# Layer 0 of a graph network kernel: one 128-edge tile of each round fetched by TensorE from a bf16 table, from round 4 on

## The chip, the cores and the metric

One core of one Trainium2 chip. The metric is the device time of one execution in microseconds. Before the change the median of 3 runs is 3726.49 us (3724.31 to 3727.02). The profiled execution took 3724.54 us, and its span (first to last instruction) is 3722.8 us.

## The reference

There are N = 6250 nodes with 96 features and 200,000 edges, sorted by their destination `dst`; `src` is random. Layer 0 is graph attention, layer 1 a weighted sum of neighbours:

```python
# layer 0
h = x @ W
e = leaky_relu((h @ att_src)[src] + (h @ att_dst)[dst], 0.2)      # self loops added
e = exp(e - segment_max(e, dst)[dst])
x = layernorm(x + tanh(segment_sum(h[src] * e / segment_sum(e, dst)[dst], dst) + bias))
# layer 1
g = gelu(x @ W_pre + b_pre)
x2 = x + segment_sum(g[src] * edge_attr, dst)
x = layernorm(x + x2 + gelu(gelu(x2 @ W1 + b1) @ W2 + b2))
```

## The kernel before, in words

Edges are taken in **groups** of 1024: 8 **tiles** of 128 edges, one edge per partition. There are 196 groups; five of them (slots 0 to 4, five buffers of everything) make a **round**, numbered 0 to 38, and group 195 stands alone at the end. `groups()` writes the order of every engine: here the first two rounds stand alone, then a hardware loop runs up to round 17, round 18 stands alone, a second loop runs to round 37, and round 38 and the last group stand alone. Because `dst` is sorted, the destinations of a group lie in a short window of nodes: 40 columns wide up to round 18 and 72 columns wide after it.

**Fetching rows.** A group needs the table row of each edge's source: 98 numbers (96 features, a one and the source's attention term). GpSimd (POOL in the profile) fetches them by indirect DMA, 8 to a group, one for each tile (L690, and for the first rounds its neighbours). Before that, SyncE's queue loads the group's `src` and `dst` (`load_edges`, L563 and L565), and for that it waits on `e0.free`, that is until the group five earlier has been summed.

**Working on a group in layer 0** is a chain over three engines, one group after the other:

- ACT (`weights`, `away`, `given`): turns the destinations into distances from the window (`far_dst` L744, eight squares L747), writes 0.2 times the scores to PSUM (L767), copies the new maxima (L769), copies the source terms from the fetched rows (L760: this one waits for the rows of the next group), and takes the exponentials (fade L776, onehot L777). L760 of the next group stands ahead of L777 of this one.
- DVE (`attend`, L1331 on): scores (L1339), maxima over the tiles (L1309), scores plus the destination's term (L1344), the maximum across partitions (L1318), its diagonal (L1319), leaky relu (L1350), candidates, new maximum, the sum of the group before (L1357, and L1359, which frees that group's slot), shifted scores (L1361), peak (L1363). Then comes L1339 of the next group.
- PE (`attend`, L999 on): sums the rows of a group, weighted, into a window of `p_acc0`: four tiles (L995), then a transposition (L989) and a broadcast (L991) of the next group's maxima, which wait for DVE, then the other four tiles (L995).

**The middle.** When the sum of 384 nodes is complete, `middle` finishes layer 0 for them and computes their rows of the table of layer 1. It stands at the end of a round, between the last group of the round and the first of the next, on all three engines (DVE begins it with L1423); a table of due times made at run time tells after which rounds. `p_node` is PSUM bank 6 and `p_node2` bank 7.

**Layer 1** already has two ways to fetch: 7 tiles of each group by GpSimd, and the eighth (the "booked" tile) by TensorE. For that the table is held in SBUF as three bf16 parts that add up to the fp32 value. DVE compares the 128 source numbers of each of the five booked tiles with the node number of each partition (L1505, 642 columns), which gives 0/1 matrices for a block of 128 nodes, and PE multiplies them with the block's three parts (L1086, 288 columns); 49 blocks cover all nodes, and DVE adds the three parts of the result (L1521).

Of the kernel before, what the change touches and what calls it, by code (L numbers as in the profile page):

```python
# [23 lines left out]
INT32 = mybir.dt.int32  # L24
# [6 lines left out]
P = 128  # L31
# [14 lines left out]
HOTS = 2  # L46


def gnn(nc, x, src, dst, edge_attr, w0, att_src, att_dst, bias0, w_pre, b_pre, w1, b1, w2, b2, out):
# [39 lines left out]
    with ctx:  # L89
# [125 lines left out]

        pair = ctx.enter_context(nc.psum_tensor("pair", [P, 2, 512], FP32))
# [61 lines left out]
        class Edge:  # L278

            def __init__(self, n):  # L280
                self.src = sems(f"e{n}_src", SLOTS)
                self.dst = sems(f"e{n}_dst", SLOTS)
                self.attr = sems(f"e{n}_attr", SLOTS)
# [4 lines left out]
                self.v = sem(f"e{n}_v")  # L288
# [16 lines left out]

        h_zero = sem("h_zero")
# [22 lines left out]
        p_top, p_topb, p_newp = bank[0][0:WIN, 0:P], bank[1][:, 0:WIN], bank[1][:, P:P + WIN]  # L329
# [5 lines left out]
        p_node, p_node2 = bank[6], bank[7]  # L335
# [55 lines left out]
        def groups(eng, body, after_round=None, alone=0):  # L391
# [11 lines left out]
            with eng.Fori(SLIM_ROUNDS, ROUNDS - 1) as it:  # L403
                one(it, WIN, WIN)
            one(ROUNDS - 1, WIN, WIN)
            return body(LAST, ROUNDS, 0, (WIN,))

        def named(it, u, ws):
            return f"{u}_{ws[0]}_{isinstance(it, int)}_{it is ROUNDS}_{first(it)}_{second(it)}"
# [7 lines left out]
        def due(eng, k, body, packed=None):  # L417

            if packed is None:
                packed = due_chunks(eng, k)  # L420
# [31 lines left out]
        def gathered(g, it):  # L452

            return 16 * (TILES * it + (LAST_T if g is LAST else TILES))

# [24 lines left out]
        def piece(c):  # L480

            return slice(PIECE[c], PIECE[c + 1])

# [24 lines left out]
        def _(sp):  # L508
# [43 lines left out]
            def load_edges(e, attrs):  # L552
                def body(g, it, u, ws):
# [3 lines left out]
                    if first(it) and not attrs:  # L557
                        return
                    if g is LAST:
# [7 lines left out]
                    if attrs:  # L567
                        sp.dma_start(attr[0:m, u, 0:t * D],
                                     edge_attr[bass.ds(g * GE, n), :].rearrange("(p j) d -> p (j d)", j=t))\
                            .then_inc(e.attr[u], 16)  # L570
                return body

            def load_booked(g, u):
                cut = P * (TILES - 1)
                sp.wait_ge(e1.free, g + 1)
                sp.dma_start(src_i[:, u, 0:TILES - 1], src[bass.ds(g * GE, cut)].rearrange("(p j) -> p j", j=TILES - 1))\
                    .then_inc(e1.src[u], 16)
                sp.dma_start(dst_i[:, u, 0:TILES - 1], dst[bass.ds(g * GE, cut)].rearrange("(p j) -> p j", j=TILES - 1))\
                    .then_inc(e1.dst[u], 16)
                sp.dma_start(dst_i[:, u, TILES - 1:TILES], dst[bass.ds(g * GE + cut, P)].rearrange("(p j) -> p j", j=1))\  # L580
                    .then_inc(e1.dst[u], 16)
# [36 lines left out]
            def load1(g, it, u, ws):  # L618
# [6 lines left out]
                if first(it) and u == SLOTS - 2:  # L625
                    sp.wait_ge(m_g, MCHUNKS + 1)
                    store_half(table1, m_st)
                    sp.wait_ge(m_g, MCHUNKS + 2)
# [9 lines left out]
            groups(sp, load_edges(e0, False), alone=2)  # L638
# [1016 lines left out]
```

## Time and profile before

| what | value |
|---|---|
| median of 3 runs | 3726.49 us |
| profiled execution | 3724.54 us |
| its span | 3722.8 us |
| busy in the span | POOL 2781.1 us, DVE 2438.3, PE 2393.6, ACT 1283.2 |
| layer 0, group loop | to about 1970 us |
| layer 1 | from about 1989 us |

PE is the matmul side of TensorE, PEld its weight loads. A row with xN stands for N instructions in one line; "mean ns" is the time of one. The time in brackets at the end of a timeline row is the idle time of the engine before it, with what ended it. The granted clock of TensorE is a share: 1.00 is 2.4 GHz and 0.50 is 1.2 GHz.

### The profile page before, as it was taken

What the parts mean: (1) busy time and instruction counts of PE and PEld (TensorE: products, weight loads), DVE (VectorE), ACT (ScalarE), POOL (GpSimd) and SP (SyncE); (2) the same over time, 40 slices, a digit from 0 to 9 for tenths busy, and PEclk for the clock granted to TensorE, in tenths of its full rate; (3) what the DMA queues carried; (4) which work ended last, traced back from release to release, by engine and by line L of the source; (5) the groups of instructions that cost most, each with busy time, mean ns of one, the idle gap of its engine ahead of it and who ended that gap; (6) DMA issues with size and microseconds to landing.
All of it is one profiled execution on the core that took longest, in us unless ns stands there. A gap on an engine that the chain in (4) does not pass through costs nothing.

```text
span 3722.8 us, 66966 instructions
## 1 busy us (share of the span) xinstructions
PE 2393.6 (64%) x16704; PEld 1951.7 (52%) x16705; DVE 2438.3 (65%) x6240; ACT 1283.2 (34%) x3893; POOL 2781.1 (75%) x2950
## 2 busy tenths in 40 slices
PE   6433343434344444444445988989888989999888
PEld 3333333333333333333334777777776777777776
DVE  7444444444466666566666777777777788888886
ACT  5433343434445555555553111111111221111222
POOL 7777777777777777777775777777777777777776
PEclk7555555555555555555557999999999999999998
DMA  5222221222222222222223343443334343444332
GB/s 102 43 42 42 41 44 42 44 42 43 42 43 44 43 44 43 43 44 45 44 45 99 93 94 90 95 94 94 95 91 96 93 96 91 97 95 99 93 95 70
DMA packets 351632, 254.26 MB, mean 68 GB/s; under 512 B 254125, under 2 KB 279218, under 8 KB 351387
## 3 DMA queue, kind: packets, MB, share of 16 engines
q0 software_dynamic: 94016, 146.16, 17.8%
q1 hardware_dynamic: 242753, 99.71, 11.7%
q10 hardware_dynamic: 14618, 6.14, 0.6%
q14 instruction: 215, 1.76, 0.2%
q8 instruction: 30, 0.49, 0.1%
HBM read 244.43 MB, written 7.25 MB: 68 GB/s over the span
## 4 chain that ended last, share of the span: by engine, by line
POOL 60%; issue 24%; ACT 4%; DVE 4%; PE 3%; DMA 2%; ACTq 1%; DVEq 1%; POOLq 0%; SPq 0%
POOL rows L690 60%; ACT onehot L747 1%; DMA rows<-table,src_i 1%; DMA src_i<-in_src_dram 1%; PE bank L1086 1%; ACT L790 1%; ACTq L740 0%; ACT pair L767 0%; DVE score L1361 0%; PE bank L1029 0%; PE bank L962 0%; ACT rowu L796 0%; DVE bst L1399 0%; ACT unused L790 0%; DVE newp L1352 0%
## 5 line engine op out<-in xcount | busy, mean ns | idle before, releaser
L690 POOL DMA_INDIRECT rows<-table,src_i x2850 | 2694.8, 946 | 896.0 <-issue 859.5
L1086 PE MATMUL bank<-node,hot 128*128 128x288 bf16 x9310 | 1228.4, 294 | 28.1 <-issue 16.5
L995 PE MATMUL bank<-onehot,rows 128*97 128x72 f32 (+1 forms) x3048 | 584.9, 369 | 814.9 <-ACT onehot L777 814.9
L1086 PEld LDWEIGHTS bank<-node,hot 128*128 128x128 bf16 x9310 | 932.2, 101 | 282.4 <-issue 20.9
L995 PEld LDWEIGHTS bank<-onehot,rows 128*97 128x97 f32 x3048 | 530.8, 281 | 854.4 <-issue 792.5
L1505 DVE TENSOR_SCALAR hot<-node,key 128x642 bf16<-128x642 int16 x1862 | 870.3, 539 | 130.8 <-PE bank L1086 80.0
L900 ACT ACTIVATE pair<-dst_i 128x8 f32<-128x8 int32 x196 | 35.2, 180 | 1175.3 <-DVE rows L1531 904.3
L747 ACT ACTIVATE onehot<-iota,far_dst 128x72 f32 (+1 forms) x1564 | 384.4, 328 | 23.0
L1339 DVE SCALAR_TENSOR_TENSOR other<-onehot,bank 128x576 f32<-128x576 f32 (+1 forms) x196 | 121.9, 622 | 404.1 <-ACT bank L760 335.4
L1073 PE MATMUL bank<-onehot,rows 128*96 128x40 f32 (+1 forms) x3128 | 306.8, 256 | 88.4 <-DVE rows L1536 50.6
L1073 PEld LDWEIGHTS bank<-onehot,rows 128*96 128x96 f32 x3128 | 295.8, 170 | 110.1 <-issue 88.7
L1531 DVE TENSOR_TENSOR rows<-rows,pair 128x672 f32<-128x672 f32 (+1 forms) x196 | 166.7, 851 | 148.5 <-DMA rows<-table,src_i 146.5
L1350 DVE TENSOR_TENSOR score<-score,pair 128x576 f32<-128x576 f32 (+1 forms) x196 | 122.2, 623 | 203.2 <-ACT pair L767 203.1
L991 PE MATMUL bank<-top_diag,ones 40*128 40x40 f32 (+1 forms) x392 | 132.3, 438 | 145.1 <-DVE top_diag L1319 143.6
L991 PEld LDWEIGHTS bank<-top_diag,ones 40*128 40x128 f32 (+1 forms) x392 | 97.9, 310 | 207.9 <-DVE top_diag L1319 205.9
L1309 DVE TENSOR_REDUCE top<-other 128x72 f32<-128x576 f32 (+1 forms) x196 | 192.5, 982 | 6.7
L760 ACT ACTIVATE bank<-rows 128x8 f32<-128x8 f32 x191 | 34.6, 181 | 440.9 <-DMA rows<-table,src_i 440.9
L790 ACT ACT_TABLE_LOAD x119 | 152.7, 1283 | 18.2 <-ACT rowt L811 11.1
L902 ACT ACTIVATE pair<-attr 128x768 f32<-128x768 f32 x196 | 156.2, 797 | 0.0
L769 ACT ACTIVATE bank<-newp 128x72 f32<-128x72 f32 (+1 forms) x196 | 43.4, 221 | 286.3 <-DVE newp L1352 286.3
L1526 DVE TENSOR_TENSOR onehot<-pair,iota 128x576 f32<-128x576 f32 (+1 forms) x196 | 121.2, 618 | 5.4 <-ACT pair L902 5.4
L1361 DVE TENSOR_TENSOR score<-score,bank 128x576 f32<-128x576 f32 (+1 forms) x196 | 121.0, 617 | 1.7
(204 smaller groups left out, 1931.1 us busy)
## 6 DMA issues: line engine op xcount, KB each, us to landing
attr<-in_edge_attr_dram SPq DMA_DIRECT2D x190, 336.0 KB
rows<-table,src_i POOLq DMA_INDIRECT x2850
node<-in_src_dram SPq DMA_DIRECT2D x195, 64.0 KB
attr<-in_edge_attr_dram SPq DMA_DIRECT2D x190, 48.0 KB
dst_i<-in_dst_dram SPq DMA_DIRECT2D x200, 4.0 KB
src_i<-in_src_dram SPq DMA_DIRECT2D x195, 4.0 KB
src_i<-in_src_dram SPq DMA_DIRECT2D x190, 3.5 KB
dst_i<-in_dst_dram SPq DMA_DIRECT2D x190, 3.5 KB
```

What stands on the lines that cost most here:

```text
L690: pool.indirect_dma_start(rows[:, u, j * width:(j + 1) * width], None, table, bass.IndirectOffsetOnAxis(ap=src_i[:, u, j:j + 1], axis=0))\
L747: last = act.activation(wide(onehot[:, u, :], w)[:, j, :], iota[:, bass.ds(lo, w)], ACT.Square, scale=FAR, bias=far_dst[:, u, j:j + 1])
L790: act.activation(unused[:, k:k + 1], zeros[0:1, 0:1], f)
L902: act.activation(p_attr, attr[:, u, :], ACT.Copy).then_inc(e1_fed, 1)
L991: pe.matmul(p_topb[:, 0:w], ones[0:w, :], top_diag[0:w, 0:w], start=True, stop=True).then_inc(t.topb, 1)
L995: last = pe.matmul(total[:, 0:w], rows0(u, it)[:, j, 0:D1], wide(weights, w)[:, j, :], start=j == 0, stop=j == most - 1)
L1073: last = pe.matmul(total[:, 0:w], rows1(u)[:, j, :], wide(hot, w)[:, j, :], start=j == 0, stop=j == most - 1)
L1086: last = pe.matmul(p_got[t], hot[:, c % HOTS, i, t * P:(t + 1) * P], tab[:, a, :, :].rearrange("p k d -> p (k d)"), start=a == 0, stop=a = ...
L1309: v.tensor_reduce(top[:, 0:w], other[:, 0:n * w].rearrange("p (j n) -> p n j", j=n), AX.X, ALU.max)\
L1350: st.step(v.tensor_tensor(by_half(score, w, n), by_half(score, w, n), p_slope(w, n), ALU.max))
L1505: last = v.tensor_scalar(hot[:, c % HOTS, i, :].rearrange("p (r e) -> p r e", r=3), src16[:, :, 0:ROW3], key[:, a:a + 1], None, ALU.is_equal)
L1531: return v.tensor_tensor(rows[:, u, 0:tiles * D], rows[:, u, 0:tiles * D], p_attr[:, 0:tiles * D], ALU.mult)
```

## The change

Layer 0 gets the same second way to fetch, for one tile per round: tile 7 of slot 0, in rounds 4 to 38 (35 rounds).

- **Table.** In rounds 1 and 2 the 49 blocks of the table (`x1`, 98 columns) are split into three bf16 parts, in 8 portions over 9 groups. ACT makes two copies and DVE two subtractions for each portion. They lie in `attr`, in a spare end of `x1` and in `hot`.
- **Sources.** SyncE's queue loads the 128 source numbers of the booked tile to all partitions, once a round (`load_src0`, behind the loads of slot 4), and ACT shortens them to int16 (`shorten_src0`, at the start of its slot 4). The loads of the booked group are split into 7 tiles and 1.
- **Marks.** DVE compares 128 columns with a [P, 1] scalar, once for each of the 49 blocks, in 10 pieces of 4 or 5 blocks: two pieces at the end of each group, for the round ahead (`marks0`). Two pieces have a buffer, so piece c waits until PE is done with piece c - 2 (`q_done`).
- **Matmuls.** PE multiplies each block, 294 columns, behind the second half of its window sum, two pieces to a group (`fetch0`), into bank 1.
- **Taking.** At the end of slot 4, DVE waits for the last piece and adds the three parts into the rows of the next round's slot 0 (`taken0`). ACT's L760 for that group waits for it.
- GpSimd gathers 7 tiles in place of 8 for that group.
- Around it: `p_topb` and `p_newp` move to bank 0, `p_node2` to bank 6 beside `p_node`, with a wait of PE on the previous chunk's GELU; no chunk is due before round 4; rounds 0 to 3 and the last two stand outside the loops; the scalar `key` is made before the loop.

```diff
-            with eng.Fori(SLIM_ROUNDS, ROUNDS - 1) as it:
+            with eng.Fori(SLIM_ROUNDS, ROUNDS - 1 - apart) as it:
                 one(it, WIN, WIN)
-            one(ROUNDS - 1, WIN, WIN)
+            for it in range(ROUNDS - 1 - apart, ROUNDS):
+                one(it, WIN, WIN)
...
+        def pieces_at(u):
+
+            return (0, 1) if u == SLOTS - 1 else (2 * u + 2, 2 * u + 3)
...
+                    if not attrs and u == SLOTS - 1 and in_era(era_at(it, u)):
+                        load_src0(it)
...
+            def load_src0(it):
+
+                if not first_era(it, SLOTS - 1):
+                    sp.wait_ge(q_src16, it + 2)
+                for k in range(BOOKED0):
+                    sp.dma_start(src_all0[:, k * P:(k + 1) * P],
+                                 src[src_rows(it + 2, k)].rearrange("(p e) -> p e", p=1).broadcast_to([P, P]))\
+                        .then_inc(q_src, 16)
...
-                    for j in range(TILES - (e is e1 and booked(it, u))):
+                    for j in range(TILES - (booked(it, u) if e is e1 else booked0(it, u, ws[0]))):
...
+                if booked0(it, u, w):
+                    act.wait_ge(q_out, it - FROM0 + 1)
                 act.activation(p_src, rows0(u, it)[:, :, D1], ACT.Copy).then_inc(t0.given, 1)
...
+            def split0(k):
+                if k > 0:
+                    act.wait_ge(h_rest, k)
+                    act.activation(table0_part(k - 1)[:, :, 1, :], table0_left(k - 1), ACT.Copy).then_inc(h_mid, 1)
+                if k < len(TABLE0):
+                    if TABLE0[k][2] is flat[2]:
+                        act.wait_ge(e0.free, 2 * SLOTS + SLOTS)
+                    act.activation(table0_part(k)[:, :, 0, :], table0_rows(k), ACT.Copy).then_inc(h_hi, 1)
...
+            def shorten_src0(it):
+
+                act.wait_ge(q_src, 16 * BOOKED0 * (it + 3 - FROM0))
+                if not first_era(it, SLOTS - 1):
+                    act.wait_ge(q_hot, (it + 2 - FROM0) * ERA0)
+                act.activation(src16_0, src_all0, ACT.Copy).then_inc(q_src16, 1)
...
+            def fetch0(it, u, c, n):
+
+                pe.wait_ge(q_hot, piece_no(it, u, c) + 1)
+                if c == 0:
+                    if first_era(it, u):
+                        pe.wait_ge(h_tab, len(TABLE0))
+                    else:
+                        pe.wait_ge(q_out, it + 2 - FROM0)
+                for i, a in enumerate(range(PIECE0[c], PIECE0[c + 1])):
+                    for t in range(n):
+                        last = pe.matmul(p_got0[t], hot0[:, c % HOTS, i, t * P:(t + 1) * P], table0_block(a),
+                                         start=a == 0, stop=a == NB - 1)
+                last.then_inc(q_done, 1)
...
                 window_sum(p_acc0, onehot[:, u, :], it, u, range(TILES // 2, TILES), w).then_inc(e0.acc, 1)
+                if in_era(era_at(it, u)):
+                    for c in pieces_at(u):
+                        fetch0(it, u, c, fetched_at(it, u, w))
 
             def middle(c, blocks=MB):
                 pe.wait_ge(m_col, c + 1)
+                pe.wait_ge(m_g, c + 1)
...
+            def taken0(it, n):
+
+                v.wait_ge(q_done, (it + 2 - FROM0) * ERA0)
+                for k in range(n):
+                    last = v.tensor_reduce(rows0(k, it + 1)[:, TILES - 1, :], p_got0[k].rearrange("p (k d) -> p d k", k=3),
+                                           AX.X, ALU.add)
+                last.then_inc(q_out, 1)
+
+            def marks0(it, u, c, n):
+
+                if c == 0:
+                    v.wait_ge(q_src16, it + 3)
+                if not first_era(it, u) or c >= HOTS:
+                    v.wait_ge(q_done, piece_no(it, u, c) - HOTS + 1)
+                for i, a in enumerate(range(PIECE0[c], PIECE0[c + 1])):
+                    last = v.tensor_scalar(hot0[:, c % HOTS, i, 0:n], src16_0[:, 0:n], key[:, a:a + 1], None,
+                                           ALU.is_equal)
+                last.then_inc(q_hot, 1)
...
                 if g is not LAST:
+                    if split_step(it, u) is not None:
+                        split_rest0(split_step(it, u))
+                    if u == SLOTS - 1 and in_era(it + 1):
+                        taken0(it, booked_in(it + 1, w))
+                    if in_era(era_at(it, u)):
+                        for c in pieces_at(u):
+                            marks0(it, u, c, fetched_at(it, u, w) * P)
+                if g is not LAST:
                     set_window(lo, after, (u + 1) % SLOTS)
```

## Rows read from the trace of the kernel before

**Rows 1.** Page of the profile, the chain that ended last, by engine.

```profile
POOL 60%; issue 24%; ACT 4%; DVE 4%; PE 3%; DMA 2%; ACTq 1%; DVEq 1%; POOLq 0%; SPq 0%
```

**Rows 2.** Stretches: busy us of PE, PEld, DVE, ACT, POOL; granted clock, DMA share, GB/s.

```profile
600.00:800.00 200.00, 80.84 (x396) 69.60 (x395) 90.15 (x298) 81.94 (x323) 151.37 (x160) 0.50 0.21 43
1200.00:1400.00 200.00, 84.79 (x413) 71.64 (x411) 126.11 (x317) 103.42 (x337) 151.24 (x161) 0.50 0.21 43
```

**Rows 3.** Groups of instructions by line, 1200 to 1900 us.

```profile
L690 POOL DMA_INDIRECT rows<-table,src_i x561 | 530.1, 945 | 171.0 <-issue 166.4 <-DMA src_i<-in_src_dram 4.6
...
L760 ACT ACTIVATE bank<-rows 128x8 f32<-128x8 f32 x69 | 12.3, 178 | 92.8 <-DMA rows<-table,src_i 92.8
```

**Rows 4.** Timeline, one group behind a middle, 1336.9 to 1344.5 us.

```profile
1336.94 0.76 DVE L1361 TENSOR_TENSOR score<-score,bank 128x576 f32<-128x576 f32 x1
...
1337.76 0.75 DVE L1339 SCALAR_TENSOR_TENSOR other<-onehot,bank 128x576 f32<-128x576 f32 x1
1337.90 0.67 ACT L777 ACTIVATE onehot<-score 128x576 f32<-128x576 f32 x1
...
1340.84 0.25 DVE L1319 TENSOR_SCALAR top_diag<-ident,top_col 72x72 f32<-72x72 f32 x1
...
1341.15 0.70 PE L991 MATMUL bank<-top_diag,ones 72*128 72x72 f32 x2 [0.67 <-DVE top_diag L1319]
...
1341.62 0.63 ACT L767 ACTIVATE pair<-score 128x576 f32<-128x576 f32 x1
1341.65 1.51 PE L995 MATMUL bank<-onehot,rows 128*97 128x72 f32 x8
...
1342.28 0.75 DVE L1350 TENSOR_TENSOR score<-score,pair 128x576 f32<-128x576 f32 x1 [1.19 <-ACT pair L767]
...
1344.43 0.75 DVE L1361 TENSOR_TENSOR score<-score,bank 128x576 f32<-128x576 f32 x1
```

**Rows 5.** Timeline around one middle, 1316 to 1347 us.

```profile
1316.17 0.42 DVE L1423 COPY colv<-acc 97x384 f32 x1 [0.61 <-issue]
...
1317.90 0.19 ACT L760 ACTIVATE bank<-rows 128x8 f32<-128x8 f32 x1 [3.45 <-DMA rows<-table,src_i]
...
1336.57 0.17 ACT L760 ACTIVATE bank<-rows 128x8 f32<-128x8 f32 x1
1336.65 0.23 DVE L1359 TENSOR_TENSOR acc<-acc,bank 97x72 f32 x1
...
1346.67 0.94 POOL L690 DMA_INDIRECT rows<-table,src_i  x1 [0.30 <-issue]
```

**Rows 6.** The chain that ended last, in order of time: start, us, what.

```profile
1337.04 2.10 DMA src_i<-in_src_dram
```

**Rows 7.** One line, L1423: the whole run, then 1010 to 1960 us.

```profile
L1423 DVE COPY colv<-acc x15: 360/421/579, 514.7 to 1918.5; 97x384 f32 x15
L1423 DVE COPY colv<-acc x12: 361/425/579, 1016.0 to 1918.5; 97x384 f32 x12
```

**Rows 8.** DVE's comparisons in layer 1 (timeline), and a 128-column operation with a scalar.

```profile
2603.43 5.54 DVE L1505 TENSOR_SCALAR hot<-node,key 128x642 bf16<-128x642 int16 x12 [0.28 <-issue]
...
L1505 DVE TENSOR_SCALAR hot<-node,key x1862: 526/539/551, 2007.8 to 3670.8; 128x642 bf16<-128x642 int16 x187
...
L1177 DVE TENSOR_SCALAR w0dst<-ones,w0att x1: 282/282/282, 9.3 to 9.3; 96x128 f32<-96x128 f32 x1
```

**Rows 9.** PE's table matmuls in layer 1 (timeline), early and late.

```profile
2011.36 4.85 PE L1086 MATMUL bank<-node,hot 128*128 128x288 bf16 x20 [7.29 <-DVE hot L1505]
...
3334.50 7.51 PE L1086 MATMUL bank<-node,hot 128*128 128x288 bf16 x60
```

**Rows 10.** Stretch of the same view as rows 2, at the start of layer 1.

```profile
2010.00:2020.00 10.00, 8.64 (x53) 6.16 (x54) 9.88 (x21) 3.35 (x6) 7.63 (x8) 0.70 0.60 143
```

**Rows 11.** DVE adding the three parts in layer 1, by line, 2100 to 3600 us.

```profile
L1521 DVE TENSOR_REDUCE node<-bank 128x96 f32<-128x288 f32 x175 | 69.9, 449 | 20.1 <-PE bank L1086 20.0
```

More of the change, by code:

```diff
@@ L389, in x_here, with groups @@
                 eng.wait_ge(s_x[-1], 16)
-        def groups(eng, body, after_round=None, alone=0):
+        def groups(eng, body, after_round=None, alone=0, apart=0):
             def one(it, w, then):
@@ L417, in due @@
         def due(eng, k, body, packed=None):
+            if isinstance(k, int) and k < HELD:
+                return
             if packed is None:
@@ L482, in piece, with in_era, narrow, booked_in @@
             return slice(PIECE[c], PIECE[c + 1])
+        def in_era(e):
+            return not isinstance(e, int) or FROM0 <= e < ROUNDS
+        def narrow(e, w):
+            return e < SLIM_ROUNDS if isinstance(e, int) else w == SLIM
+        def booked_in(e, w):
+            return BOOKED0
+        def booked0(it, u, w):
+            return in_era(it) and u < booked_in(it, w)
+        def loaded0(it, u, w):
+            if u >= BOOKED0 or (isinstance(it, int) and it < FROM0):
+                return 16 * (it + 1)
+            if booked0(it, u, w):
+                return 32 * it + 32 - 16 * FROM0
+            return 16 * (it + 1 + (SLIM_ROUNDS if u else ROUNDS) - FROM0)
+        def gathered0(g, it, u, w):
+            last = LAST_T if g is LAST else TILES
+            if u >= BOOKED0 or (isinstance(it, int) and it < FROM0):
+                return 16 * (TILES * it + last)
+            if booked0(it, u, w):
+                return 16 * ((TILES - 1) * (it + 1) + FROM0)
+            return 16 * (TILES * it + last - ((SLIM_ROUNDS if u else ROUNDS) - FROM0))
+        def fetched_at(it, u, w):
+            return booked_in(era_at(it, u), w)
+        def era_at(it, u):
+            return it + 2 if u == SLOTS - 1 else it + 1
+        def pieces_at(u):
+            return (0, 1) if u == SLOTS - 1 else (2 * u + 2, 2 * u + 3)
+        def piece_no(it, u, c):
+            return (it + (2 if u == SLOTS - 1 else 1)) * ERA0 + c - FROM0 * ERA0
+        def first_era(it, u):
+            return isinstance(it, int) and era_at(it, u) == FROM0
+        HELD = FROM0
+        SPLIT_AT = ((1, 0), (1, 1), (1, 2), (1, 3), (1, 4), (2, 1), (2, 2), (2, 3), (2, 4))
+        def split_step(it, u):
+            return SPLIT_AT.index((it, u)) if isinstance(it, int) and (it, u) in SPLIT_AT else None
+        def src_rows(e, k):
+            return bass.ds((e * SLOTS + k) * GE + P * (TILES - 1), P)
         class Steps:
@@ L558, in body @@
                         return
+                    if not attrs and booked0(it, u, ws[0]):
+                        load_split(g, u, e)
+                        return
                     if g is LAST:
@@ L637, in _ @@
             store_table()
-            groups(sp, load_edges(e0, False), alone=2)
+            groups(sp, load_edges(e0, False), alone=FROM0, apart=1)
             sp.wait_ge(e0.free, GROUPS + SLOTS)
@@ L693, in gather @@
                 return body
-            groups(pool, gather(e0, table0, D2), alone=2)
+            groups(pool, gather(e0, table0, D2), alone=FROM0, apart=1)
             pool.wait_ge(m_st, STORED)
@@ L861, in middle_due @@
                 table_for(ACT.Exp, 3)
-            groups(act, weights, middle_due, alone=2)
+            groups(act, weights, middle_due, alone=FROM0, apart=1)
             rest(act, middle, middle_last)
@@ L1037, in _ @@
             spread_top(t0, 1, SLIM)
-            groups(pe, attend, alone=2)
+            groups(pe, attend, alone=FROM0, apart=1)
             def unread(n):
@@ L1478, in _ @@
             v.wait_ge(s_w, 16 * 8)
+            v.tensor_copy(key[:, :], key_i[:, :])
             set_window(0, load_window(0), 0)
-            prev = groups(v, attend, middle_due, alone=2)
+            prev = groups(v, attend, middle_due, alone=FROM0, apart=1)
             left = due_chunks(v, ROUNDS)
@@ L1495, in _ @@
             v.sem_inc(f_var, 1)
-            v.tensor_copy(key[:, :], key_i[:, :])
             def marks(it, c):
```

117 lines of the change are left out of this document (91 added, 26 removed).

## The prediction

> **What bounds the kernel now.** The page's chain first: GpSimd's work and its issue gaps are 84% of the chain that ended last [rows 1]. The stretches of layer 0 show GpSimd equally busy in its narrow rounds and its wide ones, with TensorE's clock granted at 0.50 throughout, 1.2 GHz, while PE is busy 40 to 42% [rows 2]. By line, 561 indirect DMAs take 530.1 us and stand 171.0 us idle in between, nearly all of it issue [rows 3]: one per 1.25 us (1.248 below), 10.0 us for a group, 49.9 us for a round, with no wait that lasts. So GpSimd sets layer 0, and the other three engines follow it.
>
> How closely they follow is what decides. ACT's wait for fetched rows is 92.8 us over 69 wide groups [rows 3], 1.3 us a group: little. The timeline says why. A wide group that has fallen behind runs from L1361 to L1361 in 7.49 us [rows 4]: five are 37.4 us. A group with a middle in it, from L760 to L760, takes 18.67 [rows 5], so a middle adds 11.2 and such a round needs 48.6 of GpSimd's 49.9. There are 15 middles, 12 of them from 1010 us on [rows 7], in the 19 rounds 20 to 38, at most one to a round. GpSimd doesn't notice, because the slots are a cushion: behind a middle, L1359 frees a slot at 1336.88, the load of its sources lands at 1339.14 [rows 5, 6], and GpSimd comes to that slot at 1346.67 [rows 5]. The cushion is 7.5 us there.
>
> **Removed.** 35 indirect DMAs by 1.248 us: 43.7 us if GpSimd stays the bound. A round then has 39: 48.7 us.
>
> **Added on DVE.** 12 comparisons of 642 columns take 5.54 us, one alone 0.539 [rows 8]: they start 0.455 apart, 0.084 less than one lasts. A 128-column operation with a scalar lasts 0.282 [rows 8], so a column costs 0.50 ns and a mark 0.455 - 514 x 0.50 ns = 0.20 us apart. Bounds: 0.16, if a column costs half of that, to 0.28, if they don't overlap. I take 0.195: 0.98 for a piece of five, 1.95 for a group. Taking the parts is one reduction, 0.449 in layer 1 [rows 11], 0.37 with the same overlap.
>
> Of the column rate a page has more. The Trainium skill, "VectorE: DVE Perf Modes", What auto-detection actually checks, would give a 16-bit one-source operation with even outer dimensions four elements a cycle; by that rule a column costs half, marks come an estimated 0.165 us apart, and the sum below would come out about 12 us lower. No row here has that shape.
>
> **Added on PE.** 20 table matmuls take 4.85 us at the start of layer 1, 60 of them 7.51 later [rows 9]: 0.24 and 0.125 us each. The first is at the half clock, and 294 columns in place of 288 make it 0.245: 2.45 us for a group's ten. They come behind the second half of the window sum.
>
> **What lies beside and what on the path.** With GpSimd ahead, all of this hides: a narrow group has DVE busy 4.5 us in 10 [rows 2], 6.5 with the marks. Rounds 4 to 19 keep their gain: 16 x 1.25 = 20.0 us. The wide, lagging group is another matter, because the change closes a loop:
>
> - DVE's second piece of marks waits until PE is done with the second piece of the group before (two buffers), then 0.98;
> - from L1339 to the end of L1319: 1337.76 to 1341.09, 3.33 [rows 4];
> - from there PE's broadcast and second half: to 1343.16, 2.07 [rows 4];
> - ten table matmuls 2.45, and some 0.1 for semaphores. Sum 8.9 us.
>
> DVE's own loop is shorter: 3.33, from L1350 to L1361 2.15, from L1361 to L1339 0.82 [rows 4], marks 1.95: 8.2. Today DVE idles 1.19 before L1350, waiting for ACT's L767 [rows 4]; that idle time is the only cover, and it is used up. At slot 4 the reduction (0.37) and all marks wait for the fetch, some 0.8 more than elsewhere on balance. ACT's L760 for the next slot 0 waits for that reduction, and behind it in ACT's queue stand L776 and L777 of slot 4, for which PE's next first half waits; that is in the same 0.8. A plain round is 4 x 8.9 + 9.7 = 45.3 us, and a middle adds 11.2, plus 0.6 because L1423 now stands behind nine marks: 57.1.
>
> Against GpSimd's 48.7, a middle round overruns by 8.4 and a plain one gives back 3.4. With 11 middle rounds and 7 plain ones from 20 to 37 the followers never catch up, and the slots come free too late: GpSimd stalls. Round 38 has nothing left to fetch (48.6). The stretch costs 11 x 57.1 + 7 x 45.3 + 48.6 = 993.8, where it was 19 x 49.93 = 948.7: 45.1 more. Less the 20.0: **25 us slower, if PE keeps the half clock.**
>
> It will not always. At the start of layer 1, 4.85 us of dense matmuls came before the clock rose, and PE was busy 8.64 of 10 us at a mean of 0.70 [rows 9, 10]. In a lagging group broadcast, second half, fetch and the next first half nearly touch, so the clock should rise now and then. At the full clock the loop through PE is gone, DVE's 8.2 is left, a middle round is 53 and a plain one 42, GpSimd bounds nearly everything, and the outcome is about -27: 43.7, less some 10 us of stalls behind neighbouring middles and 6 of lag at the end. I take the full clock for a quarter of the fetches: 25 - 0.25 x 52 = **12 us slower**.
>
> **Costed at nothing.** The split in rounds 1 and 2: nine steps, each two ACT copies and two DVE subtractions of up to 686 columns. The rows with 576 columns are 0.63 and 0.75 [rows 4], so about 1.5 us on each engine; the fifth slot ahead covers it, and if it doesn't, five steps cost up to 8 us. SyncE's third load and the 64 KB broadcast per round go out on an idle queue four groups early; behind them waits only the next group's load. ACT's `shorten_src0` waits for DVE's marks and then delays slot 4's squares; that ends about when DVE does. `p_node2` with its wait: the GELU is a round old. `key` moves, 0.2 us. Longer loop bodies: no row prices them; 0 to 0.5 us a round, 0 to 17 in all, taken as 0. Layer 1 is untouched.
>
> This execution took 3724.5 us, the median is 3726.5; I put the sum on the median: 3738.
>
> **Rivals.**
> 1. **The PE clock rises and GpSimd stays the bound.** For it: nearly 5 us of PE work in one piece per group, as long as the piece that brought the clock up in layer 1. Against: PE still stands idle for about a third of each group, and a faster PE is idle sooner. About 27 us faster, 3700; 36 with marks at 0.16. Chance 0.30.
> 2. **Loop and gain cancel.** Every 0.1 us in the lagging loop is 18 x 5 x 0.1 = 9 us, so a loop of 8.8 in place of 8.9, and a clock that is full somewhat more often, end within 0.2% (7.5 us, about what this measurement can tell from no change). 0.20.
> 3. **GpSimd is held up by DVE's marks.** A diagonal (L1319) or copy beside GpSimd's work stretches DVE (L1423: 360 to 579 ns [rows 7]), while GpSimd keeps its 1.25 us [rows 3]. If it were GpSimd that waited, some 1.5 DMAs a group by half a mark, 0.2 us, in the 80 groups of rounds 4 to 19: 17 more, 29 slower, 3755. This decides from 0.25 us a group on, where the gain of rounds 4 to 19 is gone. 0.08. The Trainium skill speaks for it: "SBUF — State Buffer", Who interferes with whom, says that a vector operation in a two-port mode and GpSimd fully block each other, GpSimd's descriptor writing included. The trace agrees for DVE's side and shows nothing of it on GpSimd's.
>
> **How the numbers follow.** The forecast, the lagging loop wins, has 0.42, nearly all of it slower; with rival 3 slower is 0.50, same 0.20, faster 0.30. Slow end: marks 0.22 apart at the half clock add 11 to 25, and a few us of loop code: 3766. Fast end: the full clock, 3699. The likeliest case alone runs from 3730 to 3766.
>
> **What would show it.** Right: indirect DMAs 2815 in place of 2850 on L690's group; narrow rounds of 48.7 us; from 1000 us on, GpSimd with idle time that ends with loads of `src_i`, some 45 to 65 us in all, behind middles; wide groups behind a middle at 8.9 us; marks 0.2 apart; DVE waiting for PE before its marks; ACT's wait for rows nearly gone in the wide rounds. Wrong: a granted clock well over 0.6 in the wide part with GpSimd never waiting (rival 1); indirect DMAs over 1.25 us apart while DVE marks (rival 3); lagging groups under 8.3 us.

## The result, and the profile after

The changed kernel takes 3741.26 us (median of 6 runs, 3736.41 to 3746.19), the kernel before 3725.58 (6 runs, 3724.26 to 3727.02): 15.7 us more, ratio 1.0044, interval 1.0034 to 1.0054. The profiled execution is the slowest of the six, 3746.19, so its parts add up to some 5 us too much.

First the stretches again, the same view and columns as [rows 2], changed kernel:

```profile
600.00:800.00 200.00, 126.23 (x600) 93.18 (x600) 127.88 (x504) 86.59 (x336) 151.30 (x160) 0.57 0.23 44
1200.00:1400.00 200.00, 117.73 (x597) 86.79 (x598) 156.48 (x506) 104.11 (x336) 145.77 (x154) 0.65 0.23 43
```

In the narrow stretch GpSimd is as busy as before. In the wide one it has lost 5.5 us of 151, while DVE went from 126 to 156. What GpSimd waited for, in the whole run (engine, line, what it waited for: total us, times, longest):

```profile
POOL rows L821 <- issue: 847.7, 2780, 0.3
POOL rows L821 <- DMA src_i<-in_src_dram: 56.1, 33, 6.8
POOL rows L821 <- DMA table<-rowt: 34.3, 1, 34.3
```

33 gathers waited for `src_i`, one of them for 6.8 us: the slot came free too late, so its load started too late. The groups by line, 1200 to 1900 us, to set beside [rows 3]:

```profile
L821 POOL DMA_INDIRECT rows<-table,src_i x528 | 501.4, 950 | 195.7 <-issue 155.8 <-DMA src_i<-in_src_dram 40.0
L1534 DVE TENSOR_SCALAR hot<-node,key 128x128 bf16<-128x128 int16 x646 | 117.6, 272 | 8.9 <-PE bank L1164 6.0 <-issue 1.0
L893 ACT ACTIVATE bank<-rows 128x8 f32<-128x8 f32 x67 | 11.6, 173 | 32.0 <-DVE rows L1523 32.0
L1523 DVE TENSOR_REDUCE rows<-bank 128x98 f32<-128x294 f32 x14 | 6.5, 464 | 9.4 <-PE bank L1164 9.4
```

ACT's wait for gathered rows, 92.8 us before, is gone altogether; what is left, 32.0, is a wait for DVE's reduction of the fetched tile. The followers are now the ones that are late. A lagging wide group in the timeline (start us, us), to set beside [rows 4]:

```profile
1335.80 2.66 PE L1164 MATMUL bank<-attr,hot 128*128 128x294 bf16 x10
...
1336.31 0.74 DVE L1568 TENSOR_TENSOR score<-score,bank 128x576 f32<-128x576 f32 x1
...
1337.27 0.91 DVE L1534 TENSOR_SCALAR hot<-node,key 128x128 bf16<-128x128 int16 x5
...
1338.50 0.91 DVE L1534 TENSOR_SCALAR hot<-node,key 128x128 bf16<-128x128 int16 x5 [0.32 <-PE bank L1164]
...
1339.32 0.74 DVE L1546 SCALAR_TENSOR_TENSOR other<-onehot,bank 128x576 f32<-128x576 f32 x1
...
1342.19 0.41 DVE L1494 TENSOR_SCALAR top_diag<-ident,top_col 72x72 f32<-72x72 f32 x1
...
1342.67 0.76 DVE L1557 TENSOR_TENSOR score<-score,pair 128x576 f32<-128x576 f32 x1
...
1344.18 1.92 PE L1164 MATMUL bank<-attr,hot 128*128 128x294 bf16 x7
...
1344.81 0.75 DVE L1568 TENSOR_TENSOR score<-score,bank 128x576 f32<-128x576 f32 x1
```

From L1568 to L1568 it is 8.50 us, where it was 7.49. The five marks of the second piece begin 0.32 us late, at the end of the fetch of the group before. And the idle 1.19 us that DVE had before L1350 is gone before L1557. Slot 4 of the same round, the same view:

```profile
1360.24 2.66 PE L1164 MATMUL bank<-hot 128*128 128x294 bf16 x10
...
1362.76 0.23 DVE L1570 TENSOR_TENSOR node<-cand,node 128x72 f32 x1
1362.93 0.46 DVE L1523 TENSOR_REDUCE rows<-bank 128x98 f32<-128x294 f32 x1
...
1363.49 0.19 ACT L893 ACTIVATE bank<-rows 128x8 f32<-128x8 f32 x1 [1.63 <-DVE rows L1523]
1363.61 0.24 ACT L929 ACTIVATE fade<-drop 97x72 f32<-97x72 f32 x1
1363.76 0.67 ACT L930 ACTIVATE onehot<-score 128x576 f32<-128x576 f32 x1
1364.56 0.90 PE L1150 MATMUL bank<-onehot,rows 128*97 128x72 f32 x8 [1.67 <-ACT onehot L930]
...
1368.89 0.75 DVE L1546 SCALAR_TENSOR_TENSOR other<-onehot,bank 128x576 f32<-128x576 f32 x1 [4.03 <-issue]
```

PE's ten matmuls, DVE's reduction, ACT's copy of the next group's scores, the exponentials behind it and PE's next sum stand in a row. The last row is slot 0 of the next round: DVE has stood 4.03 us, and no semaphore ended it ("issue"). The kernel before has the same wait; of DVE's waits between 1200 and 1900 us:

```profile
DVE other L1339 <- issue: 44.8, 14, 3.7
```

There GpSimd's pace hid it. Here, with the followers late, it is on the path. The trace also records branches and register operations. In those, 3.38 us of the 4.03 lie between the branch at the end of the hardware loop's body (it ends at 1365.06 us) and the loop's first register operation (1368.44), L455 both. The view of the DMA queues for 1365.1 to 1368.4 us (packets, MB, share) has this line:

```profile
q14 instruction: 2, 0.02, 1.9%
```

That is two packets of 8 KB on the queue that the profile calls "instruction". In the wide rounds each return of the loop has such a gap (the packets are those of the returns without a middle):

| | return without a middle | packets in it | return behind a middle |
|---|---|---|---|
| before | 2.71 to 2.86 us | 1 | 2.2 to 2.7 us |
| after | 3.34 to 3.73 | 2 | 2.1 to 2.7 |
| e3, few marks | 2.75 to 2.96 | 1 | 2.2 to 2.6 |

Where no loop goes back, as into rounds 19, 37 and 38 of the changed kernel, DVE doesn't stand at all before this instruction. So the wait belongs to the loop's return, and it is longer where two packets start in it. That it is the loading of instructions fits all of this, but no run tried it by itself.

ACT's copy (L760 before, L893 now) runs once a group; its ends cut every run into parts. In us, the profiled executions of this kernel, the one before and those of the experiments below:

| | start to round 4 | rounds 4 to 19 | rounds 20 to 37 | from there to layer 1's first gather | layer 1 |
|---|---|---|---|---|---|
| before | 217.8 | 800.1 | 900.0 | 70.9 | 1733.9 |
| after | 219.7 | 782.0 | 933.9 | 70.5 | 1738.3 |
| e1, narrow rounds only | 219.6 | 782.3 | 899.5 | 70.4 | 1735.4 |
| e2, five buffers | 220.1 | 783.5 | 909.0 | 70.5 | 1734.5 |
| e3, few marks | 220.3 | 781.5 | 886.9 | 70.1 | 1734.2 |
| e4, few matmuls | 219.8 | 781.5 | 897.0 | 70.4 | 1734.7 |
| e5, two tiles | 222.0 | 856.4 | 895.2 | 70.0 | 1733.8 |
| e6, double marks | 220.3 | 803.7 | 899.8 | 70.7 | 1733.9 |
| e8, taken earlier | 220.4 | 781.9 | 893.6 | 71.5 | 1737.2 |

The change lost 1.9 us at the start, won 18.1 in the narrow rounds, and lost 33.9 in the wide ones. Layer 1's 4.4 us more belong to this execution and not to the change: its indirect DMAs stand 1.2507 us apart there, 1.2484 in the run before (mean of the undisturbed distances), and e3 and e4, with the same layer 1, take 1734.2 and 1734.7.

### The profile page after: what moved, and what is told of

Same layout as the page of the kernel before. It is cut to its first block, busy times and chain, and to the rows that moved or that the text cites. A ratio compares the mean times of both kernels' runs of the same rounds, so it can differ in the third digit from the quotient of the medians.

```text
span 3744.4 us, 72954 instructions
## 1 busy us (share of the span) xinstructions
PE 2753.9 (74%) x18419; PEld 2135.9 (57%) x18420; DVE 2754.6 (74%) x8006; ACT 1327.5 (35%) x3956; POOL 2760.5 (74%) x2915
## 4 chain that ended last, share of the span: by engine, by line
POOL 47%; issue 23%; DVE 11%; PE 10%; ACT 4%; DVEq 2%; DMA 1%; ACTq 1%; POOLq 0%; SPq 0%
POOL rows L821 47%; PE bank L1164 4%; PE bank L1150 3%; DVE hot L1534 2%; DVE other L1546 2%; DVE score L1551 1%; PE bank L1146 1%; DVEq L1451 1%; ACT onehot L878 1%; ACT L943 1%; DVE top_diag L1494 1%; ACT pair L920 1%; DVE top_col L1493 1%; DMA rows<-table,src_i 1%; DVE score L1568 0%
## 5 line engine op out<-in xcount | busy, mean ns | idle before, releaser
L1150 PE MATMUL bank<-onehot,rows 128*97 128x72 f32 (+1 forms) x3048 | 532.6, 346 | 253.7 <-ACT onehot L930 253.3
L1150 PEld LDWEIGHTS bank<-onehot,rows 128*97 128x97 f32 x3048 | 490.3, 260 | 332.5 <-issue 231.2
L1534 DVE TENSOR_SCALAR hot<-node,key 128x128 bf16<-128x128 int16 x1715 | 314.5, 276 | 43.3 <-PE bank L1164 37.9
L1144 PE MATMUL bank<-ident,top 128*72 128x128 f32 x196 | 75.1, 383 | 247.0 <-DVE top L1484 246.9
L1164 PE MATMUL bank<-attr,hot 128*128 128x294 bf16 x910 | 242.7, 449 | 0.0
L1557 DVE TENSOR_TENSOR score<-score,pair 128x576 f32<-128x576 f32 (+1 forms) x196 | 122.1, 623 | 117.1 <-ACT pair L920 115.9
L1164 PE MATMUL bank<-hot 128*128 128x294 bf16 x735 | 200.4, 450 | 0.0
L1144 PEld LDWEIGHTS bank<-ident,top 128*72 128x72 f32 x196 | 31.9, 163 | 269.7 <-DVE top L1484 266.7
L1164 PEld LDWEIGHTS bank<-attr,hot 128*128 128x128 bf16 x910 | 137.6, 157 | 66.1
```

The source lines that it names most:

```text
L1150: last = pe.matmul(total[:, 0:w], rows0(u, it)[:, j, 0:D1], wide(weights, w)[:, j, :], start=j == 0, stop=j == most - 1)
L1164: last = pe.matmul(p_got0[t], hot0[:, c % HOTS, i, t * P:(t + 1) * P], table0_block(a), start=a == 0, stop=a == NB - 1)
L1534: last = v.tensor_scalar(hot0[:, c % HOTS, i, 0:n], src16_0[:, 0:n], key[:, a:a + 1], None, ALU.is_equal)
```

## The experiments

T is the theory of the forecast: GpSimd bounds the narrow rounds, the loop of the lagging group through DVE and PE the wide ones. R1: the marks' own time on DVE is the whole price. R2: DVE's marks hold up GpSimd. R3: the splits at the start and the longer code are the price.

**A chip that had to be left out.** The first four kernels ran on a chip where the kernel before took 5391.42 us in place of 3725. Both layers are slower there: e1_narrow takes 2803 us up to layer 1's first gather and 2639 for layer 1, where the same kernel elsewhere takes 1972 and 1735.

> The fetch is kept in rounds 4 to 19 (the narrow windows) and left out of rounds 20 to 38; what the change does to the start (tables, splits) stays. T, the forecast's theory (narrow rounds are bound by GpSimd, wide rounds by the lagging group's loop through DVE and PE): the 16 narrow rounds keep 16 x 1.25 = 20 us, less the 3 us that the splits at the start cost in the changed kernel's trace, and from round 20 on the kernel is that of before: 3725.6 - 17 = 3708 to 3710 us, and the idle time of GpSimd that ends with src_i is gone from 1200 us on. R2 (the marks hold up GpSimd's DMA instructions wherever they run): the narrow rounds pay too, 3725 or more. R3 (the splits and the code are the price): about 3738.

> All as in the changed kernel, but five buffers for the marks in place of two, so that no mark waits for the previous group's fetch on PE; only the first mark group after a group 4 still waits for PE, by way of taking the fetched rows. T: in the wide rounds DVE's marks wait for PE's fetch of the group before, and PE's fetch waits for the marks; with five buffers the lagging group falls from 8.2-8.5 us to DVE's own 8.0-8.2, and the interval behind slot 4 from 11.4-11.6 to about 11.2: some 36 us back in 19 wide rounds, so 3741 - 36 = 3705 us, with 15 us of GpSimd's idle time left. R1 (the marks' own time on DVE is the price, the wait for PE lies beside it): within 5 us of 3741. R2 (marks hold up GpSimd): 3741.

> One mark in place of about five for each piece, 10 in place of 49 comparisons a round; the 49 matmuls read the first mark's block of the piece, so the fetched rows are not the table's. 39 of 49 comparisons are left out, nothing else. T: DVE has 6.4 us a round less to do and PE's matmuls remain; the two buffers still make the next marks wait for PE: 3725.6 - 30 = 3696 us. R1 (marks on DVE are the whole price): the whole of the DMAs' gain comes through, 3725.6 - 41 = 3685 us. R2 gives 3685 as well, with GpSimd's DMA instructions closer together than 1.253 us. R3 (splits, code): 3735.

> One matmul in place of about five for each piece, 10 in place of 49 a round; all 49 comparisons stay, and the fetched rows are a fifth of the table's. 39 of 49 matmuls of the fetch are left out, nothing else. T: the wait of the marks for PE falls from 1.2 us a piece to 0.25; the loop of the lagging group is then DVE's own, 8.0-8.2 us, and the interval behind slot 4 is about 10.3: 3725.6 - 30 = 3696 us, 45 us under the changed kernel. R1 (marks' own time on DVE): 3736 to 3741, little change. R2 (marks hold up GpSimd): 3741, no change.

Measured: e1_narrow 5469.57 us, ratio 1.0148 [1.0104, 1.0192]; e2_five_buffers 5541.97, 1.0261 [1.0209, 1.0313]; e3_few_marks 5548.42, 1.0275 [1.023, 1.032]; e4_few_matmuls 5493.65, 1.0156 [1.0091, 1.0221]. e2 came to the same chip again:

> [...] T: in the wide rounds the loop of the lagging group runs through DVE's wait for PE's fetch of the group before; with five buffers it falls from 8.2-8.5 us to about 8.1, and the interval behind slot 4 to about 11.2. An event-by-event recount of the rounds with the marks at the measured 0.166 us and the fetch at half clock gives 22 us faster than before, some 36 us faster than the changed kernel: 3704 us, with about 15 us of GpSimd's idle time left. R1 (the marks' own time on DVE is the price): within 5 us of the changed kernel, 3736 to 3746. R2: the same as R1.

It took 5532.03 us, before 5407.44, ratio 1.0268 [1.0194, 1.0343]. What DVE waited for between 700 and 1700 us of e1_narrow there:

```profile
DVE hot L1543 <- remote: 184.6, 31, 10.2
DVE top_col L1502 <- remote: 71.5, 16, 11.8
DVE acc L1575 <- remote: 70.1, 8, 11.1
```

Up to 10 us at a time before a mark, 31 times, for something that the trace doesn't show. PE and ACT have such gaps too, up to 12 us, and GpSimd waits up to 14.7 us for `src_i`. What causes them stays open. No theory was about this, and the order of the kernels (e3, with the fewest comparisons, is no faster than e2) fits none. These five runs decide nothing; all that follow ran where the kernel before takes 3725 to 3730.

**e1: the fetch in rounds 4 to 19 only.**

```diff
-            return not isinstance(e, int) or FROM0 <= e < ROUNDS
+            return FROM0 <= e < END0 if isinstance(e, int) else not LATE[0]
```

with END0 = 20, and rounds 20 on in a loop without the fetch.

> [...] The fetch is kept in rounds 4 to 19 and left out of rounds 20 to 38. T: the narrow rounds keep 16 x 1.25 = 20 us, less 3 us that the splits at the start cost, and from round 20 on the kernel is that of before: 17 us faster than before, 3708 to 3710 us, and GpSimd's idle time that ends with src_i is gone from 1200 us on. R2 (the marks hold up GpSimd's DMA instructions): no faster than before. R3 (the splits and the code are the price): 12 us slower than before.

Measured: 3709.41 us, before 3725.31, ratio 0.9959 [0.9945, 0.9973]: 15.9 us faster than before, in T's place. In the wide rounds GpSimd and ACT are where they were:

```profile
L830 POOL DMA_INDIRECT rows<-table,src_i x562 | 530.8, 944 | 171.3 <-issue 170.1 <-DMA src_i<-in_src_dram 1.2
L902 ACT ACTIVATE bank<-rows 128x8 f32<-128x8 f32 x70 | 12.4, 178 | 90.6 <-DMA rows<-table,src_i 90.6
```

So the whole loss comes from fetching in rounds 20 to 38. R3 falls: tables, splits and much of the code are all here. By the table they cost 1.8 us at the start.

**e2: five buffers for the marks in place of two**, the others in idle columns of `node`.

```diff
-                if not first_era(it, u) or c >= HOTS:
-                    v.wait_ge(q_done, piece_no(it, u, c) - HOTS + 1)
+                if not first_era(it, u) or c >= HOTS0:
+                    v.wait_ge(q_done, piece_no(it, u, c) - HOTS0 + 1)
```

> The kernel of e2_five_buffers, this time for a chip on which the kernel before takes its 3725 us (five buffers for the marks in place of two, all else as in the changed kernel). T: 3704 us, 22 us faster than before and 36 us faster than the changed kernel, with about 15 us of GpSimd's idle time left and lagging groups of about 8.1 us. R1 (the marks' own time on DVE is the price): 3736 to 3746. R2 (marks hold up GpSimd): the same as R1.

Measured: 3718.76 us, before 3725.95, ratio 0.9981 [0.9971, 0.9991]. 22.5 us of the changed kernel's time are back, not 36: T's direction and 0.63 of its size, and R1 falls as the whole cause. GpSimd's wait for `src_i` went from 56.1 to 25.3 us, the lagging groups from 8.21 (median of the 36 in slots 1 to 3 behind a middle) to 7.95. What stayed is slot 4 (and the return of the loop, 3.4 to 3.9 us); there, in the timeline:

```profile
1055.52 1.19 PE L1174 MATMUL bank<-hot,node 128*128 128x294 bf16 x4
1055.54 0.23 DVE L1580 TENSOR_TENSOR node<-cand,node 128x72 f32 x1
1056.74 0.47 DVE L1533 TENSOR_REDUCE rows<-bank 128x98 f32<-128x294 f32 x1 [0.97 <-PE bank L1174]
1057.13 1.55 DVE L1544 TENSOR_SCALAR hot<-node,key 128x128 bf16<-128x128 int16 x9
1057.30 0.19 ACT L903 ACTIVATE bank<-rows 128x8 f32<-128x8 f32 x1 [2.59 <-DVE rows L1533]
```

More buffers don't touch this: DVE waits 0.97 us for PE's last piece, and ACT 2.59 for DVE. The interval behind slot 4, in rounds behind a middle, is 10.92 us in the median, 10.90 in the changed kernel.

**e3: a fifth of the comparisons.** One mark a piece; 39 of 49 comparisons a round are left out.

```diff
-                for i, a in enumerate(range(PIECE0[c], PIECE0[c + 1])):
+                for i, a in enumerate(range(PIECE0[c], PIECE0[c] + 1)):
```

> The kernel of e3_few_marks, for a chip on which the kernel before takes its 3725 us: 10 of the 49 comparisons a round are done and 39 are left out, all matmuls of the fetch stay, two buffers. e2_third gave back 22 us of the changed kernel's time by taking away the wait of the marks for PE; left over against the narrow-only kernel are 10 us. T: DVE's loop for a lagging group falls from 7.96 to 7.5-7.9 us (PE's matmuls remain), GpSimd's stalls are nearly gone: 30 us faster than before, 3696 us, and the tail after the last gather of layer 0 is back near 28 us. R1 (only the marks on DVE cost): 3685. R2 (marks hold up GpSimd): 3685, with GpSimd's instructions 1.250 apart in place of 1.254. R3 (splits, code): 3735.

Measured: 3694.94 us, before 3725.98, ratio 0.9915 [0.9898, 0.9931]. T's 3696; 10 us over R1's and R2's 3685. Lagging groups take 7.56 us, slot 4 still 10.67. The edit also shortens the body of the loop, and its return takes 2.75 to 2.96 us in place of 3.34 to 3.73: over 7 plain rounds that is up to an estimated 5 us of the gain, which no theory had.

**e4: a fifth of the fetch's matmuls**, two buffers, all marks; the same edit in `fetch0`, so 39 of 49 matmuls a round are left out.

> The kernel of e4_few_matmuls, for a chip on which the kernel before takes its 3725 us: 10 of the 49 matmuls of the fetch a round are done and 39 are left out, all 49 comparisons stay, two buffers. It takes away the marks' wait for PE (as e2_third's five buffers did, 3718.8 us) and also the wait of the fetched rows for PE's last pieces behind slot 4, which e2_third keeps (11.2 us there, against 9 to 10 in e1_again). T2 (that wait is a price of its own, about 0.9 us a round in 19 wide rounds): 3696 to 3705 us, the interval behind slot 4 at about 10.3 us. R1 (what e2_third left over is the marks' own time on DVE alone): 3716 to 3719 us, as e2_third.

Measured: 3705.10 us, before 3726.58, ratio 0.9941 [0.9924, 0.9958]: T2's upper end, 14 us under e2, while R1 wanted none. Lagging groups 7.96, as in e2; slot 4 at 10.14. With the marks' wait for PE away in both, the difference is slot 4, and its remaining 2.2 us over its neighbours are not PE's.

**e6: every comparison twice**, in e1's kernel, the first into blocks that nobody reads.

```diff
-                    last = v.tensor_scalar(hot0[:, c % HOTS, i, 0:n], src16_0[:, 0:n], key[:, a:a + 1], None,
+                    for k in (HOTS, 0):
+                        last = v.tensor_scalar(hot0[:, k + c % HOTS, i, 0:n], src16_0[:, 0:n], key[:, a:a + 1], None,
```

> The narrow-only kernel of e1_again (3709.4 us) with every comparison done twice, the first time into blocks that nobody reads: 784 more marks of about 0.165 us, 129 us more of them on DVE, in rounds 4 to 19, where DVE is busy 0.64 of the time and GpSimd sets the pace. T (the marks do not hold up GpSimd, and DVE has room in the narrow rounds): 3709 to 3713 us, GpSimd's instructions still 1.250 to 1.254 us apart. R2 (a mark holds up GpSimd's DMA instructions): the time rises by the share of the marks that fall into GpSimd's part of writing descriptors; if each held it for its own length, up to 129 us more, 3838; by a third of that, 3752.

Measured: 3730.06 us, before 3724.98, ratio 1.0014 [1.0004, 1.0023]: 20.7 over e1. Both missed on the time. On the mechanism, GpSimd's DMA instructions between 270 and 740 us, those that waited for a load left out, by whether a mark ran beside them:

| | with a mark: number, mean ns, over 970 ns | without |
|---|---|---|
| e1 | 105, 951, 12 | 271, 944, 0 |
| e6 | 139, 959, 34 | 225, 946, 5 |

So marks do hold GpSimd, but by little: in these 470 us the distances beside marks add 0.7 us in e1 and 2.3 in e6. R2 is real as an effect and falls as the price. The 21.4 us lie in rounds 4 to 19, and there the narrow groups have become the bound: from round 5 to 16 a round without a middle takes 49.9 to 50.5 us, its groups 11.0, 8.8, 9.1, 9.1 and 12.2. "DVE has room" was read off its busy share; its loop had none left.

**e5: two tiles a round** in rounds 4 to 19: BOOKED0 = 2, the second sum in the bank 7, which layer 0's loop leaves idle.

> The narrow-only kernel of e1_again (3709.4 us) with two tiles of each of the rounds 4 to 19 fetched by TensorE in place of one (slots 0 and 1), the second into another PSUM bank: GpSimd issues 38 DMAs a round, 47.5 us in place of 48.7; each mark has 256 columns (by four elements a cycle 0.033 us longer than 0.163), and the fetch has 98 matmuls a round, at half clock 24 us in place of 12. T: a narrow group's loop through the two buffers and PE grows by 2.45 us, from some 6.5 to 9 us, against 9.5 us that GpSimd leaves a group, so most of 16 x 1.25 = 20 us comes through: 3690 to 3696 us. Rival: the groups that lag behind the middles of rounds 9, 13 and 16 can no longer catch up, the narrow rounds become consumer-bound like the wide ones: 3709 or more, with GpSimd waiting for src_i before 1000 us.

Measured: 3778.00 us, before 3724.98, ratio 1.0145 [1.0122, 1.0169]. The rival, and far beyond its 3709; GpSimd waits 105 us for `src_i` before 1000 us, as it said. DVE's marks and what they waited for in the whole run:

```profile
L1543 DVE TENSOR_SCALAR hot<-node,key x784: 266/282/511, 167.2 to 1030.8; 128x256 bf16<-128x256 int16 x196
its engine sat idle before it (us, times) until:
  PE bank L1173: 150.0, 123
```

That is 150 us of waits for PE. Twenty matmuls a group, 4.9 us, sit in the loop through two buffers; the interval behind slot 4 is 16.15 us, and a narrow round 54.6. Slot 4 was the term that this forecast lacked.

**e8: pieces one group earlier, taken behind slot 3**, with e2's buffers and nothing left out.

```diff
-            return it + 2 if u == SLOTS - 1 else it + 1
+            return it + 2 if u >= SLOTS - 2 else it + 1
...
-                    if u == SLOTS - 1 and in_era(it + 1):
-                        taken0(it, booked_in(it + 1, w))
                     if in_era(era_at(it, u)):
                         for c in pieces_at(u):
                             marks0(it, u, c, fetched_at(it, u, w) * P)
+                    if u == SLOTS - 2 and in_era(it + 1):
+                        taken0(it, booked_in(it + 1, w))
```

> All 49 comparisons and matmuls, five buffers as in e2_third (3718.8 us), and the schedule of the fetch moved one group forward: the first pieces of a round are marked in slot 3 of the round two before, the last in slot 2 of the round before, and DVE takes the fetched rows behind the marks of slot 3 in place of ahead of those of slot 4; the shortening on ACT and the load of the indices move with it. In e2_third DVE waits 0.97 us for PE's last piece there, and ACT's rows wait for the following group ends only with DVE's taking, so that its exponentials come late: an interval of 11.16 us behind slot 4. T3 (that chain, PE's last piece to DVE's taking to ACT's rows and exponentials, is what e2_third lost): the interval falls to 7.96 + 0.45 = 8.4 us, the 18 wide rounds take from 909 us down to near GpSimd's 48.7 us each, 877 to 885, and the tail behind the last gather shrinks: 3684 to 3695 us, faster than all kernels that leave nothing out. R4 (DVE's work for marks and taking is the price, wherever it stands): no more than the 0.97 us of DVE's wait in 18 rounds come back, 3700 to 3705 us.

Measured: 3705.90 us, before 3729.83 on that chip, ratio 0.9937 [0.9924, 0.9951]: 23.9 us faster than before. In the timeline of DVE, slots 3 and 4 of a round behind a middle:

```profile
1340.61 0.75 DVE L1579 TENSOR_TENSOR score<-score,bank 128x576 f32<-128x576 f32 x1
1341.42 1.59 DVE L1545 TENSOR_SCALAR hot<-node,key 128x128 bf16<-128x128 int16 x9
1342.93 0.45 DVE L1534 TENSOR_REDUCE rows<-bank 128x98 f32<-128x294 f32 x1
1348.78 0.75 DVE L1579 TENSOR_TENSOR score<-score,bank 128x576 f32<-128x576 f32 x1
```

The reduction waits for nobody, and the interval behind slot 4 is 8.21 us, from 10.92: T3's mechanism, and close to its number for it (8.4). The time is not T3's 3684 to 3695, and nearer R4's. 4 us are the chip (its DMAs stand 1.2502 us apart, and before took 4 more). The rest is in the wide rounds: 893.6 us, where GpSimd's own pace would be 18 x 39 x 1.2502 = 877.6. Middle rounds take 51.3 to 52.5 us. Five plain rounds, each behind a single middle, take 46.5 to 47.1 and catch up with GpSimd (their slot 3 takes 9.4 to 10.4, ACT waiting for rows). The two behind a pair of middles (32 and 35) don't, and still take 45.4 and 45.0, where five groups of 7.9 to 8.5 would be about 41: slot 0 of a plain round takes 12.1 to 13.0, with this DVE wait in it:

```profile
1355.38 0.76 DVE L1557 SCALAR_TENSOR_TENSOR other<-onehot,bank 128x576 f32<-128x576 f32 x1 [4.06 <-issue]
```

Two rounds in a row with middles (30 and 31, 33 and 34, 36 and 37) are then not made up for, and between GpSimd's last gather of layer 0 and its first of layer 1 lie 35.4 us, 28.7 before. T3's sum had left this boundary out. Of the 4.06 us, 3.61 are the return of the loop, with two packets of the instruction queue in it, as in the changed kernel. A kernel without it was not tried.

## Why the prediction was right, and where it was not

3738 was predicted and 3741 measured, "slower" had 0.50, and the mechanism was the one named: narrow rounds on GpSimd, wide rounds on their followers, GpSimd stalling behind middles. The sum was better than its terms, and that is luck: rounds 20 to 37 at the half clock were put at 46.5 us more (11 x 57.1 + 7 x 45.3, against 18 x 49.93) and cost 33.9, and the 13 us that the clock was to give back did not come.

- **Narrow rounds keep 20.0.** 18.1 kept, 17.8 in e1. The splits, costed at nothing with a bound of 8, took 1.9 us.
- **Marks 0.195 apart.** The median is 0.163, near the lower bound: the column rate of the 642-column row was carried over, and it is half that here (that row reads 3 rows of 214 columns, an odd outer dimension; a mark reads 128 in one). A piece takes 0.82 us, not 0.98. This is where the Trainium skill's "VectorE: DVE Perf Modes", What auto-detection actually checks, was right against my reading of rows: the estimate from it was 0.165. e5's 256-column marks last 0.282 us where the 128-column ones last 0.249: 0.26 ns a column.
- **The loop of 8.9.** The group shown took 8.50: 0.82 + 3.28 (1339.32 to 1342.60) + 1.58 to the start of the fetch + 2.66, and semaphores. The piece of marks (0.98 put) and PE's second half (2.07 put) were too long, the fetch (2.45 put) too short. e2 shows that the loop through PE bounds it: without the wait, 7.95, DVE's own loop (8.2 put).
- **Slot 4 costs 0.8 more.** It costs 2.7: 10.90 against 8.21 for its neighbours. This is the worst step, 1.9 us in each of 18 rounds. The chain was named, and then laid aside as "in the same 0.8". It is PE's last piece, then the reduction (0.46), then ACT's copy, the exponentials and PE's first half, one after the other. e4 and e8 separate its parts: 0.8 is PE's, 1.9 the order of ACT's and DVE's steps.
- **Rounds of 57.1 and 45.3.** Measured 54.4 to 55.5, and 46.3 to 47.7. The one is the shorter loop, less a dearer slot 4. The other is longer in spite of it: slot 4's 10.9 and four groups of 8.3 would be 44.1, but slot 0 takes 10.6 to 11.0 of a plain round. That is the DVE wait of 4 us at the loop's return, which [rows 4] (a group inside a round) don't show. "Longer loop bodies", taken as 0, made it some 0.7 us longer than before in each of the 7 plain rounds, an estimated 5 us in all. Rounds 20 to 37 cost 33.9, where 45.1 was put for 20 to 38.
- **A quarter of the fetches at the full clock: -13.** The granted clock did rise, from 0.50 to 0.65 in the wide stretch, between its levels of 1.2 and 2.4 GHz. But of 1540 distances between neighbouring fetch matmuls 7 were under 0.18 us, and the median is 0.246: the fetch got nothing of it. The window sums did. Between 1200 and 1900 us, 258 of 931 distances between their matmuls are under 0.13 us (median 0.086), where the others and all of the kernel before stand at 0.164; eight of them take 0.90 us at 1364.56 and 1.47 at 1338.25. It gave little back: e4, whose clock stays at 0.50 between 1200 and 1900 us, has lagging groups of 7.96, and e2, whose clock rises as here (0.62), 7.95. In e2 and e8, 4% of the distances in the fetch were under 0.18.
- **GpSimd idle for 45 to 65 us.** Held: 56.1 us, of which all but 33 x 0.3 = 10 is new.
- **Rival 1, the full clock:** see the point on the quarter of the fetches. **Rival 3, GpSimd held by marks:** e6 excludes it as the price, 2.3 us in 470 with twice the marks, where 17 in all was feared. The Trainium skill's "SBUF — State Buffer", Who interferes with whom, speaks of an exclusive lock that also stops GpSimd's descriptor writing. Here DVE's side shows it (a mark lasts 0.249 us in the median and up to 0.502). GpSimd's side shows it weakly: with 98 marks a round a DMA instruction beside a mark lasts 959 ns in the mean, and one without 946.

Not tried: which of the nine splits costs the 1.9 us, and a shorter or missing return of the loop.

## What to carry to other kernels

A gain on the bounding engine is worth what its followers can follow: work out each follower's loop group by group, in the rounds that already lag, and not its busy share. A result that one engine hands to the next group is dearer than its instructions, since everything behind it in the receiving queue waits too; in e8, taking it a group before it is due closed a gap of 2.7 us a round that more buffers had left open. The return of a hardware loop costs too, once the engine is on the path: look for it where the rounds meet. Where the rounds differ, a change may be right in one kind and wrong in the other: the narrow rounds alone made the first version that was faster.

## What was not expected of the hardware

- The same kernel took 5391 us on one chip and 3725 to 3730 on others, with gaps of some 10 us on DVE, PE and ACT that end with nothing the trace shows.
- A mark lasts 0.249 us and the next begins 0.163 after it: consecutive DVE operations overlap by 0.086 us.
- Marks and GpSimd's indirect DMAs stretch each other unevenly: single marks last twice their length (0.502 us), while the DMA instruction beside a mark gains 7 ns in the mean in e1 (951 against 944) and 13 in e6 (959 against 946).
- A return of the hardware loop holds DVE for 2.7 us or more, and no row of waits names it. With one 8 KB packet of the instruction queue in the gap it lasts 2.71 to 2.86 us (before, rounds without a middle), with two 3.34 to 3.73 (after).
